# Local attention: probabilities times values for four tiles in one run of TensorE, every second pair of tiles

## What is computed

```
q = x Wq / sqrt(dh);  k = x Wk;  v = x Wv
g = sums of x over 16 tokens;  side_k = g Wk;  side_v = g Wv
keys of a block of 128 queries: its own block, the one before, the one after, and the 64 side keys
logits = q . keys + bias      (|key - query| <= 127 is allowed)
m = max(max(logits), 0);  p = exp(logits - m) / (sum exp(logits - m) + exp(-m))
y = p . values;  out = y Wo
```

## Time and profile before

| | |
|---|---|
| median of 3 runs | 1858.35 us (1856.60 to 1860.22) |
| the profiled execution, device time | 1853.26 us |
| its span | 1851.5 us |
| PE busy | 1793.2 us (97%) |
| PE weight loads | 1286.7 us (69%) |
| DVE busy | 1077.8 us (58%) |
| ACT busy | 925.4 us (50%) |
| POOL busy | 562.4 us (30%) |
| mean granted clock of TensorE | 0.986 |

### The profile page before, as it was taken

The page is one execution under the profiler, slowest core; times in us unless marked ns, Lnnn a source line. Parts: engine busy times, 40 slices in busy tenths (PEclk is TensorE's granted clock), DMA queues, the critical chain, the costliest instruction groups (busy, mean ns, idle before and its releaser), DMA issues.

```text
span 1851.5 us, 41363 instructions
## 1 busy us (share of the span) xinstructions
PE 1793.2 (97%) x17153; PEld 1286.7 (69%) x17153; DVE 1077.8 (58%) x2319; ACT 925.4 (50%) x1697; POOL 562.4 (30%) x966
## 2 busy tenths in 40 slices
PE   7999999999999998999999999999999999999997
PEld 3666778665757656777777777766777777777775
DVE  5684644261242257888888788843555544445454
ACT  2313231213243236888888888854555544445512
POOL 3262130042130352212111121113555544445413
PEclk8979999999999999999999999999999999999999
DMA  6100002113353576601012010000000000010001
GB/s 190 26 24 1 4 1 76 67 57 114 103 182 93 178 208 133 110 21 42 22 42 99 23 40 23 21 24 2 2 2 2 2 1 2 2 31 2 2 0 46
DMA packets 90476, 93.55 MB, mean 51 GB/s; under 512 B 35314, under 2 KB 75698, under 8 KB 90162
## 3 DMA queue, kind: packets, MB, share of 16 engines
q1 hardware_dynamic: 84034, 79.13, 15.2%
q0 software_dynamic: 3456, 9.44, 1.9%
q10 hardware_dynamic: 2800, 2.34, 0.4%
HBM read 67.82 MB, written 23.07 MB: 49 GB/s over the span
## 4 chain that ended last, share of the span: by engine, by line
PE 90%; DVE 4%; ACT 2%; DMA 1%; issue 1%; POOL 1%; POOLq 0%; SPq 0%; DVEq 0%; ACTq 0%
PE PS L1871 13%; PE PS L1249 8%; PE PS L1885 7%; PE PS L1258 7%; PE PS L2210 6%; PE PS L1862 6%; PE PS L2288 5%; PE PS L2265 4%; PE PS L2215 3%; PE PS L2249 3%; PE PS L615 3%; PE PS L707 2%; PE PS L2295 2%; PE PS L102 2%; PE PS L2327 2%; PE PS L714 2%
## 5 line engine op out<-in xcount | busy, mean ns | idle before, releaser
L2044 DVE CUSTOM_DVE_ANT_0 arena<-PS,arena 128x1024 f32<-128x1024 f32 x256 | 312.1, 1220 | 60.5 <-PE PS L1862 56.5
L1965 ACT ACTIVATE arena<-arena 128x1024 f32<-128x1024 f32 x256 | 296.8, 1159 | 9.3 <-DVE arena L2044 9.1
L1871 PE MATMUL PS<-arena 128*128 128x128 f32 x2048 | 278.7, 279 | 0.4 <-ACT arena L1961 0.2
L1871 PEld LDWEIGHTS PS<-arena 128*128 128x128 f32 x2048 | 229.5, 142 | 60.2 <-issue 27.0
L2492 POOL TENSOR_SCALAR arena<-arena 128x384 f32<-128x384 f32 (+1 forms) x256 | 142.8, 569 | 252.0 <-DVE arena L2401 251.9
L2373 ACT ACTIVATE arena<-arena 128x385 f32<-128x385 f32 (+1 forms) x256 | 151.5, 594 | 128.7 <-DVE arena L2410 128.7
L1961 ACT COPY arena<-PS 128x512 f32<-128x512 f32 x298 | 169.9, 585 | 62.2 <-PE PS L1871 59.7
L1862 PE MATMUL PS<-arena 96*128 96x512 bf16 x512 | 154.3, 383 | 4.9 <-DVE arena L2044 3.8
L2410 DVE CUSTOM_DVE_ANT_0 arena<-PS,arena 128x384 f32<-128x384 f32 (+1 forms) x256 | 123.2, 538 | 52.2 <-PE PS L2252 39.8
L2051 DVE COPY arena<-PS 128x512 f32<-128x512 f32 x214 | 147.0, 687 | 3.7 <-PE PS L1871 3.5
L1249 PE MATMUL PS<-arena 128*128 128x512 f32 x320 | 141.5, 599 | 6.6 <-ACT arena L1394 5.9
(11 more groups left out here) (340 smaller groups left out, 3076.9 us busy)
## 6 DMA issues: line engine op xcount, KB each, us to landing
arena<-in_L_ffn_W SPq DMA_DIRECT2D x16, 1024.0 KB, 7.3
arena<-prior SPq DMA_DIRECT2D x16, 512.0 KB, 4.0
parts<-arena SPq DMA_DIRECT2D x24, 256.0 KB, 5.6
arena<-parts SPq DMA_DIRECT2D x96, 64.0 KB, 2.9
arena<-parts SPq DMA_DIRECT2D x48, 128.0 KB, 8.1
prior<-arena SPq DMA_DIRECT2D x4, 1024.0 KB, 6.4
ye<-arena SPq DMA_DIRECT2D x7, 512.0 KB, 3.0
ya<-arena SPq DMA_DIRECT2D x7, 512.0 KB, 4.9
```

Source lines behind the costliest of these rows:

```text
L1871: h = e.transpose(PS[:, i, P * j:P * j + P], Sb[z % 3][:, 512 * g + P * j:512 * g + P * j + P], ident)
L1965: e.activation(Sb[z % 3], Sb[z % 3], ACT.Exp, bias=mr[:, z % 4:z % 4 + 1], scale=-1.0).then_inc(s_exp, 1)
L2044: e.tensor_tensor_reduce(Sb[z % 3], ps, Ab[m % 2], 1.0, 3e38, ALU.add, ALU.min, mr[:, z % 4:z % 4 + 1]).then_inc(s_ttr, 1)
```

## The change

The values of four tiles are put in one run. In steps 2 and 6 TensorE does values(z-6) to values(z-3); in steps 0 and 4 it does none. So that the probabilities can wait longer, Pt gets eight places (four more in memory that lies idle: yT[1] during the first batch, X4T[0] during the second), and VM gets seven. The waits on s_val follow: the copies of turn(z) wait for values(z-4) in place of values(z-2), and GpSimd for values(z-7) in place of values(z-4). Nothing is computed more or less.

```diff
     Pt = [arena.up(384) for _ in range(4)]
+    Pt_more = [[flat(z)[:, 384 * j:384 * j + 384] for j in range(4)] for z in (yT[1], X4T[0])]
     sm, mr = arena.up(8), arena.up(8)
-    VM = [arena.up(2 * P).rearrange("p (a c) -> p a c", a=2) for _ in range(4)]
+    NV = 7
+    VM = [arena.up(2 * P).rearrange("p (a c) -> p a c", a=2) for _ in range(NV)]
+
+    def weights_of(x):
+        j = x % 8
+        return Pt[j] if j < 4 else Pt_more[x // 128][j - 4]
...
-                    h = e.matmul(PS[c, YB, o + lo:o + hi], wt[:, c], Pt[(2 * z + d) % 4][:, P * j + lo:P * j + hi], start=m == 0, stop=m == len(work) - 1)
+                    h = e.matmul(PS[c, YB, o + lo:o + hi], wt[:, c], weights_of(2 * z + d)[:, P * j + lo:P * j + hi], start=m == 0, stop=m == len(work) - 1)
...
-            for y in (z - 4, z - 3):
-                if y >= 0:
+            if z % 4 == 2 and z >= 6:
+                for y in range(z - 6, z - 2):
                     values(y)
...
-            w.wait_ge(s_val, z - 1)
-            e.copy(Pt[2 * z % 4], PS[:, 4, 0:384]).then_inc(s_tc[0], 1)
+            w.wait_ge(s_val, z - 3)
+            e.copy(weights_of(2 * z), PS[:, 4, 0:384]).then_inc(s_tc[0], 1)
...
-            w.wait_ge(s_val, z - 1)
-            e.tensor_copy(Pt[(2 * z + 1) % 4], PS[:, 5, 0:384]).then_inc(s_tc[1], 1)
+            w.wait_ge(s_val, z - 3)
+            e.tensor_copy(weights_of(2 * z + 1), PS[:, 5, 0:384]).then_inc(s_tc[1], 1)
...
-            u, t, vm = z // 8, z % 8, VM[z % 4]
-            w.wait_ge(s_val, z - 3)
+            u, t, vm = z // 8, z % 8, VM[z % NV]
+            w.wait_ge(s_val, z - NV + 1)
```

More of the change, by code:

```diff
@@ L2270, in values @@
             u, n = z // 8, z // 4
-            v, k0, vm = v5[u % 2], first_key(z), VM[z % 4]
+            v, k0, vm = v5[u % 2], first_key(z), VM[z % NV]
             for d in range(2):
```

## The result

| | before | after |
|---|---|---|
| median of 6 runs | 1857.79 us (1856.60 to 1861.61) | 1866.32 us (1862.41 to 1869.72) |
| ratio to before | | 1.0042, 95% interval 1.0028 to 1.0056 |
| the profiled execution | 1853.26 us | 1864.52 us |
| its span | 1851.5 us | 1862.4 us |

By the ratio the changed kernel is slower by 0.42%, 7.8 us, with an interval of 5.2 to 10.4 us; the two medians lie 8.5 us apart. The forecast was 7.1 us slower, 1865.4 us, with a range of 1859.5 to 1870.0; the median measured, 1866.32, lies inside it.

The account below looks back on a forecast made before the run. PE (TensorE), 97% busy, bounds the kernel, so only the spacing of its groups counts; -0.2 (steps 0 and 2), +5.0 (steps 4 and 6), +2.2 and +0.1 (last unit) sum to +7.1 us: 1865.4 us, range 1859.5 to 1870.0.

Parts of the forecast that it names:

- Where the second turn goes: Steps 0 and 4: turn(z-1) waits for ScalarE's copy, starting 4.16 and 4.44 us after first score, losing 0.32 and 0.43.
- Steps: Lengths of an attention unit's four steps: 6.7, 9.7, 5.2 and 7.55 us, 29.2 where it was 28.85.
- the join of two runs: Steps 2 and 6: values put next to another run save one tiling switch, 0.115 us per four tiles.
- A pair of steps 0 and 2: Units 1 to 14: step 0 shrinks 1.42 us, step 2 grows 1.405, pair worth -0.015.
- a pair 4 and 6: Units 0 to 14: step 4 shrinks 1.02 us, step 6 grows 1.385, pair costs +0.365 without a projection.
- Steps with a projection: Four of the steps 4: the projection behind the turn loses a 0.13 us wait, so the pair costs +0.235.
- the second chunk: Step 0: no longer waits for the first chunk's copy; chunk to next scores 1.82 us instead of 1.91.
- Last unit: No chunks: removing values from steps 0 and 4 gains nothing, steps 2 and 6 grow 1.1 us each, end +0.1.
- The drain alone: Rival: in attention only saved tiling switches count, -3.6 us and perhaps another -3.1, 1851.7 to 1854.7 us; chance 0.06.
- VectorE held by bank YB: Rival: VectorE's copy of bank YB delays recip and the next turn, +9 us on top, 1874 us; chance 0.06.
- The wash: Rival: attention losses stand, but dearer switches and half the last unit's cost leave +3.4 us, 1861.7; chance 0.16.
- Costs set at nothing: Attention: other memory for Pt, looser waits and VectorE's later copy of bank YB were each taken to cost nothing.

Follow-up runs that it names:

- the repeat: The changed kernel run once more with nothing altered; ratio 1.0041 to the kernel before, attention stage 495.27 us.

## Why the prediction was right, point by point

- **Where the second turn goes** was the core of it, and held to 0.01 us: 4.17 and 4.45 after the first score, forecast 4.16 and 4.44. It could be read because one step of the trace of before (z = 2) already was a step without values. The time at which TensorE could have gone on, forecast at 3.84 and 4.01, is what the kernel with both copies earlier shows (3.84 and 4.02). The forecast looked at ScalarE's copy alone; VectorE's, 0.15 us ahead of the transposes that need it, happened not to decide, and the forecast had not looked whether it would.
- **Steps.** Forecast 6.69 and 9.71, measured 6.69 and 9.68; forecast 5.24 and 7.55, measured 5.25 and 7.52. The long step was forecast 0.03 too long each time: the join of two runs saves more than the 0.115 us that I read. From first value to first transpose the run of four takes 2.87 us (1415.16 to 1418.03) where the two runs took 1.52 + 1.49 = 3.01, so 0.14. A pair of steps 0 and 2 gained 0.05, not 0.015, a pair 4 and 6 lost 0.34, not 0.365.
- **Steps with a projection**: forecast +0.235 for the pair, measured 8.72 - 10.01 + 1.35 = +0.06. Most of the difference is that the projection, when it need not wait, is itself 0.1 us shorter (3.56 us in place of 3.66 to the next score), as I had allowed for the second chunk and not here.
- **Last unit**: its steps 120 and 124 stayed at 4.97 and 5.25 as forecast. Its step 126 with the end grew by 12.41 - 11.17 = 1.24 (forecast 1.1 + 0.1). Its step 122 grew by 2.70, not 1.1: the later turns are there (6.38 at full clock, +1.13), but the fall of the clock, 1.6 us, was in no term and no rival.
- **The sum** is therefore right in part by luck. Measured: 14 x -0.05 = -0.7, then 11 x 0.34 + 4 x 0.06 = +4.0 (forecast 5.0), then +3.9 for the last unit (forecast 2.3): 7.2, the stage shows 7.12. The pairs were set 1.5 us too dear, the clock's 1.6 us were missing, and by chance the two cancel. In the repeat, with two falls, it is 8.7.
- **Rivals.** The drain alone (-3.6 and more): the switches were worth 31 x 0.14 = 4.3 us, and the waits for the copy, 14 x 0.32 + 15 x 0.43 = 10.9 us, took more than that back. VectorE held by bank YB: excluded by the late copy of that bank. The wash needed dearer switches and half of the last unit's +2.2; switches are dearer, by a quarter, but the last unit paid all of it. (The prediction calls this rival's switch twice as dear and reckons with 0.20 in place of 0.115; twice would have given 1 us less.)
- **Costs set at nothing** (places, waits, VectorE's hold) were nothing: 0.04 us for the places, no change for the hold in any step of units 0 to 14.

## What to carry to other kernels

Work that stands on the busiest engine between two steps of a chain may be cover for a queue on another engine. Before moving it, put next to each other the time at which the busy engine could go on and the time at which the copy behind it ends, step by step; here 3.84 and 4.01 against 4.16 and 4.44 us. And if the move pays only with a copy further forward, move every copy that the same step waits for: a trace names as releaser the one that decided, and not the one that would decide next.

## What the runs showed of the hardware

- The granted clock fell to its lower level (1.2 GHz) for 3.4 us around the end of step 120 in all five traces that have no values there and not both copies moved forward (in the changed kernel busy for 3.09 of 4.97 us, no single wait over 2.1 us), and around the end of step 124 (busy for 3.20 of 5.25) in four of the five. With values left in step 120 (busy 4.62 of 4.97) it did not. If the idle time is the cause, as I take it to be, a wait that is free by the dependencies cost 1.6 us this way. With both copies earlier the same step is shortened to 3.77 us with the same work, and the clock held.
- A change of the array's tiling costs about 0.14 us here (0.14 saved by a join, 0.12 to 0.17 paid for each one added). Behind values a first chunk takes 0.1 us longer than behind a turn, with 512 columns (1.82 against 1.72 us) as with 128 (1.89 against 1.79).
